# A selective-scan layer: the next batch's front in another order over the sixteen states

## What is computed

```python
xz = x @ in_proj_w.T
xi, z = jnp.split(xz, 2, axis=-1)                  # 128 channels each
xc = conv1d(xi.transpose(0, 2, 1), 4 taps) + conv_b
xs = silu(xc)
dt, Bm, Cm = jnp.split(xs @ x_proj_w.T, [4, 4 + 16])
delta = softplus(dt @ dt_proj_w.T + dt_proj_b)
for t in range(1024):                              # for each of 16 states n
    h = exp(delta[t] * A) * h + (delta[t] * xs[t]) * Bm[t]
    y[t] = sum over n of h * Cm[t]
y = (y + xs * D) * silu(z)
out = y @ out_proj_w.T
```

## Time and profile before

| | |
|---|---|
| median of 3 runs | 414.72 us (414.06 to 416.75) |
| span of the profiled execution | 398.3 us |
| busy: PE, DVE, POOL, ACT | 306.8, 308.8, 281.8, 235.3 us |
| scans of DVE (L1305, 58 instructions) | 119.8 us |
| products of POOL (L509, 64) | 143.9 us |
| sums of PE (L973, 256) | 127.6 us |
| units 0, 1, 2, 3 begin on DVE at | 31.71, 96.61, 164.76, 239.33 us |
| last tiles begin | 289.08 us |

### The profile page before, as it was taken

One profiled execution on the slowest core, in us unless ns is written; L12 is line 12 of the kernel. 1 busy time (PEld: TensorE's weight loads), 2 busy tenths in 40 slices (PEclk: granted clock), 3 DMA queues, 4 the chain that ended last, 5 costly groups with the idle time before them and its releaser, 6 DMA issues. The chain is left out here.

```text
span 398.3 us, 4350 instructions
## 1 busy us (share of the span) xinstructions
PE 306.8 (77%) x1257; PEld 180.7 (45%) x1257; DVE 308.8 (78%) x360; ACT 235.3 (59%) x519; POOL 281.8 (71%) x201
## 2 busy tenths in 40 slices
PE   7832978675996988589799769579879569999940
PEld 3311423222644343264434426346458446898940
DVE  4799995999899969878994789999998315667630
ACT  4456696723888595387849774746566135546320
POOL 3435845989696459989973999997688702477771
PEclk9965898989999799889869978999898859999975
DMA  5187999999688935858994366799931073000000
GB/s 102 31 278 258 265 270 343 416 216 381 256 281 285 363 122 183 316 194 275 320 322 166 111 235 208 268 305 365 288 84 31 15 199 79 4 16 18 21 12 0
DMA packets 43986, 78.68 MB, mean 198 GB/s; under 512 B 16050, under 2 KB 26093, under 8 KB 43962
## 3 DMA queue, kind: packets, MB, share of 16 engines
q1 hardware_dynamic: 41066, 73.88, 56.9%
q0 software_dynamic: 2896, 4.53, 4.1%
HBM read 72.30 MB, written 7.54 MB: 200 GB/s over the span
## 5 line engine op out<-in xcount | busy, mean ns | idle before, releaser
L509 POOL TENSOR_TENSOR prod<-h,csb 128x1024 f32<-128x1024 f32 (+1 forms) x64 | 143.9, 2254 | 34.4 <-DVE h L1305 12.4
L973 PE MATMUL Yp<-prod,ident 128*128 128x512 f32 (+1 forms) x256 | 127.6, 630 | 30.5 <-POOL prod L509 30.5
L1305 DVE TENSOR_TENSOR_SCAN h<-dA,Bp 128x1024 f32<-128x1024 f32 (+2 forms) x58 | 119.8, 2065 | 14.4 <-ACT dA L691 10.1
L973 PEld LDWEIGHTS Yp<-prod,ident 128*128 128x128 f32 x256 | 49.7, 207 | 91.5 <-issue 45.4
L1264 DVE TENSOR_TENSOR Bp<-Cp,bsb 128x1024 f32<-128x1024 f32 (+1 forms) x58 | 67.8, 1168 | 6.2 <-DMA bsb<-bc_rows 4.0
L691 ACT ACTIVATE dA<-delta,aneg 128x1024 f32<-128x1024 f32 (+1 forms) x58 | 62.9, 1095 | 12.7 <-DVE h L1305 8.3
L605 POOL DMA_INDIRECT out_dram<-dA,csb x30 | 30.0, 1002 | 28.3 <-DVE dA L1495 20.0
L548 POOL DMA_INDIRECT slots<-rows_,slot x30 | 30.2, 1005 | 6.6 <-issue 4.3
L1140 PE MATMUL Cp<-prod,w1s 128*128 128x384 f32 (+1 forms) x64 | 21.6, 462 | 0.0
L1154 PEld LDWEIGHTS Bp<-w2s,prod 128*128 128x128 f32 x152 | 18.1, 192 | 1.8 <-issue 0.3
L1481 DVE TENSOR_TENSOR dA<-Bp,b2s 128x320 f32<-128x320 f32 (+1 forms) x8 | 3.8, 475 | 19.2 <-PE Bp L1154 19.2
(11 more groups left out here) (289 smaller groups left out, 605.8 us busy)
## 6 DMA issues: line engine op xcount, KB each, us to landing
bsb<-bc_rows SPq DMA_DIRECT2D x48, 512.0 KB, 6.5
csb<-bc_rows SPq DMA_DIRECT2D x48, 512.0 KB, 5.8
bsb<-bc_rows SPq DMA_DIRECT2D x16, 384.0 KB, 5.9
csb<-bc_rows SPq DMA_DIRECT2D x16, 384.0 KB, 6.9
slots<-fill POOLq DMA_DIRECT2D x1, 2600.0 KB, 24.2
csb<-slots SPq DMA_DIRECT2D x6, 325.0 KB, 5.0
bcs<-bc_rows SPq DMA_DIRECT2D x2, 512.0 KB, 12.3
xs_in<-in_x_dram SPq DMA_DIRECT2D x1, 768.0 KB, 5.5
```

Source lines behind the costliest of these rows:

```text
L509: po.tensor_tensor(prod[:, k % 4, c], h[:, k % 3, c], csb[:, k % CSLOTS, c], ALU.mult).then_inc(s_pP, 1)
L973: ins = te_.matmul(Yp[:, c], idn, prod[:, k % 4, c], start=False, stop=(n == 15), skip_group_check=True)
L1305: ins = ve.tensor_tensor_scan(h[:, k % 3, c], decays, drives, h[:, k % 3, c.start - 1:c.start] if i else 0.0, ALU.mult, ALU.add)
```

## The change

Seven edits of order, with the same arithmetic:

1. ACT: the bias is added to half 0 of the convolution as before; half 1 goes through Silu directly from PSUM, in step 4, behind the Silu of half 0. `f_xcr` counts one per batch, `f_silu` as before. The Silu of the last `sz` and the table loads move with it from step 5 to 4.
2. PE and ACT: the step's projection and softplus come first (steps 5 to 8, small terms in 9), the rows of B and C behind (steps 8 and 9), the gate's halves a step earlier on ACT (10 and 11). The waits on the shared bank `M0` follow that order.
3. POOL and DVE: the front's stages each a step earlier (9, 10, 12, 13; select in 11). SP stores the rows at step 12, not 10.
4. `place`: back's stages 7 to 10 come one step later on PE, ACT and DVE in units 1 to 3.
5. `turned`: ACT copies the first half of the first transposes in step 4, the second in step 5.
6. PE: in steps above 4 the sum of state n - 1 comes ahead of back and front (behind back's stage 5 in step 5), and sum 15 ahead of the next front's transposes in step 0.
7. ACT: batch 3's `sz` gets its Silu in unit 3, step 7, with its own table switch, not in unit 2, step 12.

```diff
--- before.py
+++ after.py
@@ -298,6 +298,15 @@
...
+def turned(v, n):
+    first = 4 if v < CARRY else 5
+    return (n - first,) if n in (first, first + 1) and quad(v, n - first) else ()
+def place(v, n):
+    return {7: (), 8: (7,), 9: (8,), 10: (9,), 11: (10,)}.get(n, (n,)) if v < CARRY else (n,)
 def logits(v, nt):
@@ -415,7 +424,7 @@
...
                 bring_B(v, n + 2)
-            if n == 10 and v + 1 < B:
+            if n == 12 and v + 1 < B:
                 store_rows(v + 1)
@@ -509,18 +518,18 @@
...
     def front(f, n):
-        if n == 10:
+        if n == 9:
             pool.wait_ge(f_ln, f + 1)
             po.tensor_tensor(tabs[:, :], yt_free[:, :], tabs[:, :], ALU.subtract).then_inc(f_less, 1)
-        if n == 11:
+        if n == 10:
             po.tensor_tensor(trel[:, :], trel[:, :], ex[:, :], ALU.add).then_inc(f_high, 1)
-        if n == 13:
+        if n == 12:
             pool.wait_ge(f_pick, f + 1)
...
             po.tensor_tensor(at(delta, f), trel[:, :], tabs[:, :], ALU.subtract).then_inc(f_delta, 1)
-        if n == 14:
+        if n == 13:
             pool.wait_ge(f_delta, f + 1)
@@ -625,19 +634,20 @@
...
                               ACT.Identity, bias=bcol[:, :], scale=gcol[:, :]).then_inc(f_top, 1)
-        if n in (3, 4):
-            q = n - 3
-            act.wait_ge(f_mx, 2 * f + q + 1)
+        if n == 3:
+            act.wait_ge(f_mx, 2 * f + 1)
             if f >= 2:
                 act.wait_ge(b_yg, f - 1)
-            ac.activation(at_half(u, f, q), bank(f, "conv", q), ACT.Identity, bias=cb[:, :]).then_inc(f_xcr, 1)
-        if n == 5:
+            ac.activation(at_half(u, f, 0), bank(f, "conv", 0), ACT.Identity, bias=cb[:, :]).then_inc(f_xcr, 1)
+        if n == 4:
+            act.wait_ge(f_mx, 2 * f + 2)
             act.drain()
-            ac.activation(at(u, f), at(u, f), ACT.Silu).then_inc(f_silu, 1)
+            ac.activation(at_half(u, f, 0), at_half(u, f, 0), ACT.Silu)
+            ac.activation(at_half(u, f, 1), bank(f, "conv", 1), ACT.Silu, bias=cb[:, :]).then_inc(f_silu, 1)
             ac.activation(at(sz, f - 1), at(sz, f - 1), ACT.Silu).then_inc(f_gate, 1)
...
         for q in range(2):
-            if n == 6 + q:
+            if n == 8 + q:
                 act.wait_ge(f_bc, 2 * f + q + 1)
@@ -648,37 +658,32 @@
...
                           scale=BAR, bias=-BAR).then_inc(bars, 1)
-        if n in (7, 8):
-            q = n - 7
+        if n in (5, 6):
+            q = n - 5
             act.wait_ge(f_dt, 2 * f + q + 1)
...
             ac.activation(trel[:, HB[q]], bank(f, "step", q), ACT.Relu, bias=dtb[:, :]).then_inc(f_am, 1)
-        if n == 8:
+        if n == 6:
             act.drain()
             ac.activation(ex[:, :], tabs[:, :], ACT.Exp, scale=-1.0)
+        if n == 7:
             act.drain()
             ac.activation(yt_free[:, :], ex[:, :], ACT.Copy, bias=1.0)
-        if n == 9:
             act.drain()
             ac.activation(tabs[:, :], yt_free[:, :], ACT.Ln)
+        if n == 8:
             ac.activation(yt_free[:, :], yt_free[:, :], ACT.Copy, bias=-1.0).then_inc(f_ln, 1)
             act.wait_ge(p_bx, sum(x < f for x, _ in POOLED))
             ac.activation(te[:, :], ex[:, :], ACT.Square, scale=0.5 ** 0.5)
+        if n == 9:
             ac.activation(small[:, :], ex[:, :], ACT.Relu, scale=-255.0 * 1024.0,
                           bias=edge[:, :]).then_inc(f_sq, 1)
-        if n in (11, 12):
-            q = n - 11
+        if n in (10, 11):
+            q = n - 10
             act.wait_ge(f_mz, 2 * f + q + 1)
...
             ac.activation(at_half(sz, f, q), M0[:, :], ACT.Copy).then_inc(f_zr, 1)
-        if n == 12 and f == B - 1:
-            act.drain()
-            ac.activation(at(sz, f), at(sz, f), ACT.Silu).then_inc(f_gate, 1)
-            act_set()
         if n == 15:
@@ -736,7 +741,7 @@
...
                 ins.then_inc(b_n2, 1)
-        for q in parts(v, n, 5):
+        for q in turned(v, n):
             w = quad(v, q) * P
@@ -839,12 +844,16 @@
...
                 carry(n - 1)
-            if v and n != 8 and n < 10:
+            if v and n < 8:
                 back(v - 1, n)
...
                 front(v + 1, n)
-            if v and (n == 8 or n >= 10):
-                back(v - 1, n)
+            if v == CARRY and n == 7:
+                ac.activation(at(sz, B - 1), at(sz, B - 1), ACT.Silu).then_inc(f_gate, 1)
+                act_set()
+            if v and n >= 8:
+                for stage in place(v - 1, n):
+                    back(v - 1, stage)
     for n in range(8):
@@ -935,26 +944,25 @@
...
                        stop=True).then_inc(f_mx, 1)
+        if n in (8, 9):
+            q = n - 8
+            if q == 0:
+                pe.wait_ge(f_am, 2 * f)
+            else:
+                pe.wait_ge(f_row, 2 * f + 1)
+            te_.matmul(bank(f, "rows", q), bcT[:, :, :].rearrange("p k r -> p (k r)"), at_half(u, f, q),
+                       start=True, stop=True).then_inc(f_bc, 1)
         if n in (5, 6):
...
                 pe.wait_ge(f_silu, f + 1)
-            else:
-                pe.wait_ge(f_row, 2 * f + 1)
-            te_.matmul(bank(f, "rows", q), bcT[:, :, :].rearrange("p k r -> p (k r)"), at_half(u, f, q),
-                       start=True, stop=True).then_inc(f_bc, 1)
-        if n in (6, 7):
-            q = n - 6
-            if q == 0:
-                pe.wait_ge(f_row, 2 * f + 2)
             else:
...
             if q == 0:
-                pe.wait_ge(f_am, 2 * f)
+                pe.wait_ge(f_row, 2 * f + 2)
             else:
@@ -1098,25 +1106,24 @@
...
         for n in range(16):
-            if n in (5, 11):
-                if v:
-                    back(v - 1, n)
-                    if n == 11:
-                        back(v - 1, 12)
+            if n == 0 and v:
+                add_state(v - 1, 15)
+            if n > 4:
+                if v and n == 5:
+                    back(v - 1, 5)
                 add_state(v, n - 1)
-                if v and n == 5:
-                    back(v - 1, 6)
+                if v and n > 5:
+                    for stage in place(v - 1, n):
+                        back(v - 1, stage)
             if v + 1 < B:
...
                 if n == 4:
-                    pe.wait_ge(f_xcr, 2 * v + 1)
-            if n == 0 and v:
-                add_state(v - 1, 15)
-            if v and n not in (5, 6, 11, 12):
-                back(v - 1, n)
-            if n and n not in (5, 11):
+                    pe.wait_ge(f_xcr, v + 1)
+            if 0 < n < 5:
+                if v:
+                    back(v - 1, n)
                 add_state(v, n - 1)
@@ -1251,7 +1258,7 @@
...
     def front(f, n):
-        if n == 12:
+        if n == 11:
             dve.wait_ge(f_less, f + 1)
```

## The result

The changed kernel takes 426.68 us (median of 4 runs, 424.52 to 431.68) against 414.59 us (414.06 to 416.75, 4 runs): ratio 1.0258, 95% interval 1.0207 to 1.0308. It is 2.6% slower. I had forecast 411.0 us and a range up to 418. The profiled execution has a span of 425.3 us and took 427.06 us, so only 1.8 us lie outside the span, not the 16.4 us that I had taken from the kernel before.

A forecast was written before the change was run, and what follows sets the result against it. DVE's idle time, from a ring PE to ACT to POOL to PE to ACT to DVE, was the bound; -4.3 and +0.5 us on the 398.3 us span gave 394.5, plus 16.4 outside it 411.0 us, range 402 to 418.

The forecast's parts named there:

- Sum 15 ahead of the transposes: PE, step 0: DVE's 1.28 us wait for the gating goes, ACT's copies end 1.9 us later; gain given back, 0.6 more.
- The sum of unit 1: Walk through unit 1 by PE, ACT, POOL and DVE: first drive of unit 2 at 165.5, 0.8 us later than before.
- Silu block: ACT, one state earlier: block of 4.9 us ahead of decay 7, so the scan of state 7 newly waits 1.65 us.
- Softplus and POOL: ACT takes 12.6 us from Silu block to last softplus input, 5.4 us earlier; on POOL that becomes 0.7.
- Waits ahead of s14: End of units 1 and 2: DVE waits some 3 us for the logits, behind sum 10, products and gate.
- No decay wait at s11 and s12: DVE's scans of states 11 and 12: decays 8 to 13 in time, the 10.1 us of decay waits go.
- Last Silu later: ACT, unit 2 to unit 3: 3.6 us gone ahead of unit 2's 3.52 us softmax wait; costs 0 in unit 3.
- Store at SP's step 12: SP's store of the rows waits until about 140.6, read 24 us on by the next unit: cost 0.
- What lies outside the span: Median 414.72 us is 16.4 above the profiled span of 398.3; left as it is and added to the forecast.
- B: PE's clock falls in new gaps, 4.7 us idle before product 9: 4 to 5 us lost each unit, 420 us; chance 0.13.
- A: More slack than assumed: no 3 us logits waits in units 1 and 2; gain 10.8, 404 us; chance 0.25.
- C: No effect: every wait removed returns at the next engine; 414 us; chance 0.22.

The follow-up runs named there:

- e2: Kernel before with one edit alone, sum 15 ahead of the transposes in PE's step 0; 428.32 us, ratio 1.0334.
- e3: Changed kernel with three extra matmuls that no result needs in PE's step 1, ahead of its wait for ACT's copies; 422.0 us, ratio 1.0039.
- e10: Kernel before with two edits only, the Silu block in step 4 and the last Silu in unit 3; 415.50 us, ratio 0.9925.
- e9: e1 with back's stages 7 to 10 in their old steps; 418.37 us (11 runs), ratio 0.9933.
- e5: Kernel before with the last Silu alone moved to unit 3, step 7; 414.24 us, ratio 0.9954.
- e8: Changed kernel, unedited, run and profiled again; 427.2 us, ratio 1.0275.
- e4: e1 with the sums of steps 10 and 11 behind back and front again; 414.18 us, ratio 0.9991.
- e11: e9 and e4 together: back's stages in old steps, sums of steps 10 and 11 behind back and front; 421.68 us, ratio 1.0136.
- e1: Changed kernel with one edit undone, sum 15 behind the next front's transposes again; 416.56 us, ratio 0.9978.
- e6: e1 with all sums behind back and front but that of step 5; 414.94 us (four runs), no ratio.
- e7: e1 with four matmuls of no use in PE's step 10, ahead of sum 9; 419.39 us, no ratio.
- b0_again: Kernel before, unchanged, profiled again; 419.54 and 424.39 us, ratio 1.0145.

## Why the prediction was wrong, point by point

**Sum 15 ahead of the transposes: the step that failed.** I priced it as "the gain is given back, and 0.6 more", by durations of the earlier trace rows at full clock, and never asked what PE does while ACT copies. It waits 2.80 us. Then the 14.7 us in which "PE is serial from the end of those copies" took their length from a trace in which that gap was 0.54. The measured chain from copies' end to the copy of ACT behind it is 107.2 to 126.55, 19.3 us: my 14.7, and 10.5 instead of 5.9 for the three slow operations, 4.6 more. e2 and e3 show it from both sides. The later start was in my sum (1.9 us); the slow clock behind the gap was not, and stood in no term of it.

**The sum of unit 1, redone.** I had d0 of unit 2 at 165.5; it is 174.34. The terms: copies end at 107.2 and not 105.1, since p15 of unit 0 is 2.5 us later than in the earlier trace rows (2.1; which edit makes it late no run singles out); the clock in the first gap (4.6); transposes to last softplus input 18.3 us as against my 18.2 (0.1); from there to s14 21.5 us, where I had 19.8, sum 9 at half clock (1.7); s14 to d0 8.1 us, not 7.75 (0.4). That makes 8.9 of 8.8 us. Unit 2 starts 8.4 us late on my walk's clock and loses 5.3 more, of which its own slow stretches (2.97 + 3.67 + 3.73 instead of 5.9, and 3.78 for sum 9: 6.3 us) give 4.6, as 1.7 us were in my number already. The other 0.7 us are not accounted for.

**Silu block.** s7 waits 2.26 us in unit 1 and 2.26 in unit 2; I had 1.65. The halves take 0.63 and 0.67 us (0.6 and 0.7 expected), the block 127.21 to 131.97, 4.8 us (4.9 expected). Right as a mechanism for this order; in e10, where the block starts at 117.20, there is no such wait. The next activation stands 1.30 us behind the load's start, so the drain of the Trainium skill's page ("ScalarE: Activation LUTs", What ACT_TABLE_LOAD costs) isn't seen here either.

**Softplus and POOL.** ACT's 12.6 us from block to last input and "5.4 become 0.7" can't be read by clock times, as all is shifted; by intervals the first was right (131.97 to 144.76, 12.8 us), and so was the second: POOL's first operation starts at 144.85, the four end with p10 at 154.1 (151.76 and 2.35), 9.3 us, as against 9.4.

**Waits ahead of s14.** 3.98 and 3.78 us against "some 3 us", and for the reason given: gate and products stand behind the late sum. The place of back's stages is part of the cause: e9 undid it and the wait went. But other waits came in its place and the units kept their length, so the wait was not worth what it showed.

**"No decay wait at s11 and s12".** Right for these two; a wait that I had not foreseen stands at s13, 1.21 us in unit 1 and 1.75 in unit 2. The yt wait was to go and is 1.90 us in unit 1, because p15 was late, and gone in unit 2.

**Last Silu later.** Right: no wait of DVE for it in unit 3, and in e5 worth 2.2 us at its own place.

**Store at SP's step 12: "cost 0" was wrong in unit 0.** SP's queue has the late weights behind the store, some 9 us of issuing (7.27 of them for one table), and then the first loads of unit 1. I looked at unit 1 only, where nothing is behind it. SP in after:

```profile
77.46 0.32 SPq L392 DMA_DIRECT2D bc_rows<-bcs  x1
...
81.94 7.27 SPq L388 DMA_DIRECT2D b2s<-in_L_ffn_b_dram  x1
```

In the kernel before, that long issue starts at 78.53. The first drive of unit 1 now waits for its row of B: 0.57 us in after, 1.13 in e8, 2.61 in e3, about 1 in e4 and e11, 0.49 in e9, nothing in e1, e6 and e7; and nothing in any profile with the old place (before, b0_again, e2, e5, e10).

**What lies outside the span.** Wrong as a reading, harmless in the sum: the difference of the loops (first drive of the last tiles at 289.08 before, 300.27 after, 11.2 us) is nearly the difference of the medians, 12.1. That they agree is in part luck: in b0_again, a longer execution, the last tiles begin at 296.36, 3.9 us ahead of after.

**The rivals.** B had the mechanism and the sign: PE's clock falls in a gap that the new order opens, 420 us. I placed it only at the gap ahead of sum 9, where it cost 1.9 us a unit (e7 filled it, and the slow stretch went to the next sums), and not at the first one, where it cost 4.6. By my own figure, 1.9 us a unit, the gain was gone with the second gap alone. The price that I put on B was loose too: half of 7.3 us is 3.7, not 4 to 5. I gave it 0.13. For this the Trainium skill ("TensorE: Matmul & The Clock Gate", Part 1: idle PE is throttled, activity releases it) spoke more clearly than I let it. The trace agrees on the first half, with 3.67 us behind the gap for what takes 2.00; on the second it is less plain, as PE then worked for some 10 us with hardly a pause before sums took 1.88 us again. A had no base: the slack was eaten before the ring got to s7. C, every removed wait comes back at the next engine, describes the other edits once the sum is back in its place: e1, 416.56 us, ratio 0.998. As forecasts A and my case had the wrong sign, and C had no effect where there was a loss of 12 us.

## What to carry to other kernels

Before moving work out of a gap, look at what else is left for that engine in it: on PE the next stretch can cost more (4.6 us) than the wait that was to be removed (1.28 us). Price each reordering of PE at both clock levels, and walk the first gap as carefully as the one that the change is about. Take the time outside the span from two profiles, not from one, and look at a moved DMA in every pass of the loop, since one pass may have other transfers queued behind it.

## What was unexpected of the hardware

PE idle for 2.8 us with 4.13 us of work in the 7 us before was followed by about 10 us at clock 0.52, although PE was busy for 10.05 of those 10.3 us. After 2.80 us the three operations took 10.5 to 10.7 us in unit 1 of each of the profiles (after, e8, e2) and 10.2 to 10.4 in unit 2. With a gap of 0 to 0.54 us in unit 1 (e3, e10, before) they took 5.9, all at full clock. With 1.08 to 1.09 us they came out every way, from 5.9 (e4, e11) to 9.3 us (e6), as the table above has it. Nor is this gap all that counts: in unit 2 of e3 it is filled, and they took 7.7 us; PE had waited 1.98 us for a product some 7 us before. The runs of the kernel before spread from 410.9 to 424.9 us in one group and from 412.2 to 430.5 in another; that its middling gap sometimes costs the clock and sometimes not would be part of an explanation, and after, with 2.80 us, does repeat better (424.5 to 431.7 in eight runs), but no run here shows that this is the whole of it.

Left open is how the loss of after divides between the later start and the clock, and whether any mix of the edits beats the kernel before by more than a measurement can tell. e10 (0.9925) and e9 (0.9933) come nearest; both intervals end just below 1, both are within 1%, and the kernel before missed itself by more in b0_again.
